# Two attention layers on one core: softmax chain, ends of the halves, offsets and keys one step later in the plan

## The reference

```
xn   = x * bn1_g' + bn1_b
q    = grouped 1x1 conv(xn)                        # 8 groups of 16 channels
off  = tanh(pw(gelu(conv6x6_stride4(q)))) * 4      # 8x8 offsets per group
grid = (8x8 positions + off), scaled
kv   = bilinear sample of xn at grid;  k, v = grouped 1x1 convs of kv
pos  = query grid - key grid;  f = sign(pos) * log1p(|pos|)
bias = relu(relu(f @ w1 + b1) @ w2 + b2) @ w3 + b3 # 2 -> 32 -> 32 -> 1, per query and key
attn = softmax(q k / 4 + bias);  x = x + out_w (attn v) + out_b
x    = x + mlp_w2 gelu(mlp_w1 bn2(x) + mlp_b1) + mlp_b2
```

## Time and profile before

| | us |
|---|---|
| three runs | 893.63, 896.69 (median), 896.9 |
| profiled execution | 898.17 |
| its span, first to last instruction | 896.4 |
| PE, DVE, ACT busy in the span | 811.4, 717.5, 676.1 |
| mean granted TensorE clock | 0.981 of full speed |

### The profile page before, as it was taken

The page is one execution under the profiler, slowest core; times in us unless marked ns, Lnnn a source line. Parts: engine busy times, 40 slices in busy tenths (PEclk is TensorE's granted clock), DMA queues, the critical chain, the costliest instruction groups (busy, mean ns, idle before and its releaser), DMA issues.

```text
span 896.4 us, 27521 instructions
## 1 busy us (share of the span) xinstructions
PE 811.4 (91%) x12470; PEld 232.1 (26%) x12470; DVE 717.5 (80%) x530; ACT 676.1 (75%) x775; POOL 3.1 (0%) x7
## 2 busy tenths in 40 slices
PE   2299998889999999888999999988999999999997
PEld 1122222222222222222222222222222222222224
DVE  4789799798877589898885869979888668989843
ACT  2468778978777688896776877797878678888863
POOL 1000000000000000000000000000000000000000
PEclk8599999999999999999999999999999999999999
DMA  4502010020110201002020200102002020200000
GB/s 163 120 2 49 3 39 12 12 65 3 43 34 1 48 3 49 12 14 54 1 63 15 49 1 14 37 12 56 12 3 61 14 48 2 72 3 3 2 15 24
DMA packets 18264, 27.67 MB, mean 31 GB/s; under 512 B 10980, under 2 KB 11620, under 8 KB 18148
## 3 DMA queue, kind: packets, MB, share of 16 engines
q1 hardware_dynamic: 18148, 25.91, 11.7%
HBM read 23.05 MB, written 2.74 MB: 29 GB/s over the span
## 4 chain that ended last, share of the span: by engine, by line
PE 67%; ACT 15%; DVE 8%; issue 7%; DMA 2%; SPq 1%; ACTq 0%
PE pair L870 23%; PE scores L888 22%; ACT h L467 8%; PE pair L844 6%; DVE h L621 4%; PE pair L1023 3%; PE scores L899 3%; PE pair L978 2%; PE pair L996 2%; PE pair L1014 2%; DVE big L725 2%; PE scores L984 1%; PE pair L923 1%; ACT big L569 1%; ACT L569 1%
## 5 line engine op out<-in xcount | busy, mean ns | idle before, releaser
L621 DVE TENSOR_TENSOR h<-hxy 128x2048 f32<-128x2048 f32 x256 | 578.1, 2287 | 77.2 <-PE pair L870 73.2
L467 ACT ACTIVATE h<-pair 128x1024 f32<-128x1024 f32 x512 | 517.6, 1024 | 143.4 <-PE pair L844 104.6
L870 PE MATMUL pair<-h,wts 32*32 32x512 f32 x8192 | 299.9, 603 | 19.5 <-ACT h L467 5.5
L888 PE MATMUL scores<-h,wts 128*32 128x512 f32 x2048 | 275.6, 607 | 0.1
L844 PE MATMUL pair<-fy,u_rows 32*128 32x512 bf16 x1024 | 102.8, 387 | 15.3 <-DMA fy<-fy_dram 15.3
L870 PEld LDWEIGHTS pair<-h,wts 32*32 32x32 f32 x8192 | 65.9, 103 | 81.2 <-ACT h L467 35.1
L844 PEld LDWEIGHTS pair<-fy,u_rows 32*128 32x128 bf16 x1024 | 26.5, 91 | 232.6 <-issue 232.6
L888 PEld LDWEIGHTS scores<-h,wts 128*32 128x32 f32 x2048 | 42.1, 108 | 157.3 <-issue 148.2
L748 DVE TENSOR_REDUCE neg_max<-pair 128x8 f32<-128x512 f32 x32 | 22.1, 691 | 22.8 <-PE pair L978 22.8
L978 PE MATMUL pair<-const,probs 128*128 128x128 f32 x128 | 20.5, 284 | 21.6 <-ACT h L467 20.8
L477 ACT ACTIVATE probs<-scores,wts 128x512 f32<-128x512 f32 x32 | 22.0, 688 | 23.7 <-PE scores L888 23.5
(11 more groups left out here) (99 smaller groups left out, 341.3 us busy)
## 6 DMA issues: line engine op xcount, KB each, us to landing
hxy<-features_dram SPq DMA_DIRECT2D x64, 256.0 KB, 4.9
wts<-weights_dram SPq DMA_DIRECT2D x2, 960.0 KB, 7.9
att_den<-reciprocals_dram SPq DMA_DIRECT2D x7, 256.0 KB
x<-x_dram SPq DMA_DIRECT2D x2, 512.0 KB, 5.5
fy<-fy_dram SPq DMA_DIRECT2D x16, 64.0 KB
fy_dram<-fy_part SPq DMA_DIRECT2D x24, 32.0 KB, 3.7
out_dram<-x SPq DMA_DIRECT2D x3, 256.0 KB, 5.4
features_dram<-pos_sign SPq DMA_DIRECT2D x4, 128.0 KB, 2.3
```

The source lines that it names most:

```text
L467: emptied("z", 2 * g + j, act.activation(h2[j][g % H2_BUFS][:].rearrange("p r n -> p (r n)"), pair_of("z", 2 * g + j)[:], ACT.Relu))
L621: dve.tensor_tensor(h1[g % H1_BUFS][:].rearrange("p c (y x) -> p c y x", x=W), hx[unit % 2][:, :, t].unsqueeze(2).broadcast_to([128, CT, H ...
L870: ins = pe.matmul(z_of(g, r)[32 * c:32 * (c + 1)], w(l, "w2")[key_rows(r), key_rows(r)], h1[g % H1_BUFS][key_rows(r), c], start=r >= 2, st ...
L888: ins = pe.matmul(scores[phase % 2][32 * r:32 * (r + 1)], w(l, "w3")[:, 32 * t:32 * (t + 1)], h2[rows[0] // 2][step % H2_BUFS][:, r % 2], ...
```

## The change

Numbers in the plan's tables go up by one. The softmax stages move from steps 2, 3, 4 of the following phase to 3, 4, 5 on all three engines; all stages of the end of a half move by one step; of the work for the next segment only `offset`, `offset_tanh` (35 to 36) and `keys_values`, `keys_values_out` (51 to 52) move. `fy_weights` of the second layer moves from DVE step 21 to 22. `copy_scores`, `queries_keys`, `hidden_terms`, the other stages for the next segment, the first segment's own slots and the tail's table keep their steps. No instruction is added or removed, and SP's list of DMAs is the same.

```
-    ("dve", "conv_sum", 1): 34, ("act", "conv_gelu", 0): 33, ("pe", "offset", 0): 35,
-    ("act", "offset_tanh", 0): 35, ("dve", "positions", 0): 38, ("pe", "spread", 0): 37,
+    ("dve", "conv_sum", 1): 34, ("act", "conv_gelu", 0): 33, ("pe", "offset", 0): 36,
+    ("act", "offset_tanh", 0): 36, ("dve", "positions", 0): 38, ("pe", "spread", 0): 37,
...
-    ("pe", "attend", 0): 5, ("act", "attend_out", 0): 5, ("dve", "reciprocal", 0): 9, ("dve", "divide", 0): 12,
+    ("pe", "attend", 0): 6, ("act", "attend_out", 0): 6, ("dve", "reciprocal", 0): 10, ("dve", "divide", 0): 13,
...
-SOFTMAX_SLOTS = {("pe", "scores_t"): 2, ("dve", "score_max"): 4, ("act", "widen_max"): 3,
-                 ("pe", "max_off"): 4, ("act", "exp"): 4}
+SOFTMAX_SLOTS = {("pe", "scores_t"): 3, ("dve", "score_max"): 5, ("act", "widen_max"): 4,
+                 ("pe", "max_off"): 5, ("act", "exp"): 5}
...
-    put("dve", 21, "fy_weights", 1)
+    put("dve", 22, "fy_weights", 1)
```

More of the change, by code:

```diff
@@ L85 @@
     ("dve", "hat_products", 0): 46, ("dve", "hat_products", 1): 47, ("pe", "sample", 0): 48, ("dve", "sample_out", 0): 50,
-    ("pe", "keys_values", 0): 51, ("act", "keys_values_out", 0): 51,
+    ("pe", "keys_values", 0): 52, ("act", "keys_values_out", 0): 52,
 }
 AFTER_SLOTS = {
-    ("pe", "attend", 0): 5, ("act", "attend_out", 0): 5, ("dve", "reciprocal", 0): 9, ("dve", "divide", 0): 12,
-    ("pe", "project", 0): 12, ("dve", "residual1", 0): 14, ("pe", "mlp_up", 0): 14, ("act", "mlp_gelu", 0): 14,
-    ("pe", "mlp_up", 1): 15, ("act", "mlp_gelu", 1): 15, ("pe", "mlp_down", 0): 17, ("dve", "residual2", 0): 19,
-}
-SOFTMAX_SLOTS = {("pe", "scores_t"): 2, ("dve", "score_max"): 4, ("act", "widen_max"): 3,
-                 ("pe", "max_off"): 4, ("act", "exp"): 4}
+    ("pe", "attend", 0): 6, ("act", "attend_out", 0): 6, ("dve", "reciprocal", 0): 10, ("dve", "divide", 0): 13,
+    ("pe", "project", 0): 13, ("dve", "residual1", 0): 15, ("pe", "mlp_up", 0): 15, ("act", "mlp_gelu", 0): 15,
+    ("pe", "mlp_up", 1): 16, ("act", "mlp_gelu", 1): 16, ("pe", "mlp_down", 0): 18, ("dve", "residual2", 0): 20,
+}
+SOFTMAX_SLOTS = {("pe", "scores_t"): 3, ("dve", "score_max"): 5, ("act", "widen_max"): 4,
+                 ("pe", "max_off"): 5, ("act", "exp"): 5}
 TERMS_SLOT = 12
```

## The result

The changed kernel takes 900.22 us, the median of 20 runs (893.73 to 907.11). The kernel before, timed beside it 20 times, takes 896.73 us (893.63 to 899.48). The ratio is 1.004, with an interval of 1.0023 to 1.0057: slower by 3.5 us, with the whole interval above 1, where 889.4, a gain of 7.3, was forecast. The time lies outside the range of 885 to 896 and on the other side.

The account below looks back on a forecast made before the run. PE bounds the kernel, busy 811.4 of 896.4 us, its largest wait in the steps before the scores' transposes. Terms -5.0 + 0 - 0.8 + 0 - 1.5 - 0.9 + 0.5 + 0.4 = -7.3 give 889.4 us, range 885 to 896.

Parts of the forecast that it names:

- plain phases: Transposes one step later see an undisturbed ACT: 0.28 us gained in each of 18 phases, -5.0 us (0 to -8.3).
- L1023 and MLP's first matmuls: MLP's second matmuls inherit the transposes' wait, net 0 in six phases; its first matmuls lose waits, -0.8 us.
- features: Three segments: wait before transposes splits, PE waits some 2.4 us before features instead of 1.1; net 0 (-6.2 to +6.2).
- distances and hats: Three segments: DVE waits 0.7 to 0.8 us for the transposes instead of 1.34; -1.5 us (0 to -3.8).
- second layer's weights: PE's 0.86 us wait for a first layer standing behind these weights goes: -0.9 us (0 to -0.9).
- `q`: Loses the subtraction in front of it and gets a 0.18 us wait, three times: +0.5 us (0 to +0.5).
- DVE's maximum: Comes a step later with more slack behind it, softmax stages keep their distances: counted at nothing.
- tail: Attend of the last-but-one half starts a step later, delaying divide and last reduction: +0.4 us (0 to +2.2).
- clock falls: Rival: every long PE wait drops the clock, 1.7 us each; three falls 892.8 (chance 0.06), nine places 903.0 (0.04).
- I count one such fall before and one after: Clock term: number of half-rate falls in the steps unchanged, 0 us (-1.7 to +5.1, for none and four).
- three falls and 892.8: Rival case: the three longer waits before the features alone drop the clock, two falls more than now; chance 0.06.
- layer2 waiting for DVE's reduction: Listed sign that the forecast is wrong: PE's layer2 held until DVE has done its reduction; no size given.

Follow-up runs that it names:

- e1: Changed kernel plus eight matmuls by zero weights filling PE's wait behind `spread` in each later segment; 899.27 us, ratio 1.0029 to the kernel before.
- e9: Changed kernel with the hidden terms one step later (13), but at step 12 in the three units over the hats; 893.86 us, ratio 0.9962 to before.
- e5: Changed kernel with hidden terms later except at hats, features' exponential behind the features, last-but-one half and its softmax at their old steps; 887.82 us, ratio 0.9885 to before.
- e7: e1 with the last-but-one half and last-but-one phase back at the steps of before; 894.04 us, ratio 0.9958 to the kernel before.
- e11: Changed kernel with only the last-but-one half and last-but-one phase back at the steps of before, no filling; 898.05 us, ratio 1.0019 to before.
- e8: Kernel before plus eight matmuls by zero weights ahead of the transposes behind the offset convolution's GELU, three times; 894.69 us, ratio 0.9975 to before.
- e2: Changed kernel with the hidden terms one step later (13 in place of 12) everywhere; 898.43 us, ratio 1.0011 to the kernel before.
- e3: Changed kernel with `offset` and `offset_tanh` back at step 35; 897.17 us, ratio 1.0013 to the kernel before.
- e4: Changed kernel with offsets and the softmax of the features' and distances' phases in their old slots; 897.67 us, ratio 1.0005 to the kernel before.
- e6: e5 plus eight matmuls by zero weights behind `spread`; 889.35 us, ratio 0.9911 to the kernel before.

## Why the prediction was wrong

Its terms, by phases at full clock (before and e1):

| Term | forecast | measured |
|---|---|---|
| plain phases, 18 | -5.0 | 18 x -0.21 = -3.8 (21.83 to 21.62) |
| L1023 and MLP's first matmuls | -0.8 | -1.0 (phases 65, 73 and 81: 86.43 to 85.88, less a plain phase's 0.21, three times) |
| features | 0 | 3 x +0.10 = +0.3 (28.62 to 28.72) |
| distances and hats | -1.5 | 3 x -0.54 = -1.6 (27.35 to 26.81) |
| second layer's weights | -0.9 | -0.8 (23.22 to 22.18, less 0.21) |
| `q` | +0.5 | 3 x +0.28 = +0.8 (24.71 to 24.78, and the 0.21 that it hides) |
| last phase of the steps | 0 | -0.2 (21.42 to 21.20) |
| DVE's maximum | 0 | 3 x (0.40 + 1.22) = +4.9 |
| sum of the steps | -7.7 | -1.4; measured directly -1.5 |
| tail | +0.4 | +0.5 |
| clock, at the median | 0 | +4.8 |

In the rows of L1023 and `q` the reduction's wait, which e9 and e5 are free of, is taken out and stands in its own row.

*The clock* was the first step to fail. The text knew the mechanism: it had the rival "clock falls", and even a time for nine of them, 903.0. In the profile the clock fell at six of its nine places, at the features and at the transposes of the distances; behind the GELU, where the wait had split into 0.58 and 0.52 us, it did not. The text gave the rival one in ten, since "five of the six waits of 1.65 us and more left the clock up". That reading took waits of 1.65 and 2.05 us for the measure of one of 2.62. The step "I count one such fall before and one after" failed at the size: in the profiled execution it is eight stretches of 3.4 us in these six places, 1.26 us each (10.1 / 8), and 4.8 us at the median. The profiles of e1 and after and the times of e7 and e11 show the cause, since only PE's idle time behind `spread` was filled. The Trainium skill (TensorE: Matmul & The Clock Gate, Part 1: The HAM clock gate) says that the half rate is the default and that activity releases it. The runs agree: none of the six places that e1 and e7 fill dropped the clock, nor the three of e8, while 8 of the 12 waits of 2.62 us in the profiles of after, e2, e9 and e11 (3, 2, 2 and 1 of three each) did. By that rule the text had three falls and 892.8; there were more, since PE was slowed again at the transposes of the distances and two of the falls behind the features lasted 6.8 us. Why a given wait drops the clock in one place and not in the next stays open, and its length is not the whole of it: of the waits of 2.9 us in e3 one of three did.

*The maximum on DVE* was the second. "The maximum on DVE comes a step later too, with more slack behind it": the slack is on the side of its consumer on ACT, but the reduction also empties a PSUM pair, for which layer2 waits. I followed the value and not the buffer. In the new order the reduction had moved past the hidden terms; among the distances I used this to find a gain, and did not look what it does in the other phases. e9 takes back 4.9 us by one slot. This sign was among those that I had listed as wrong: layer2 waiting for DVE's reduction.

*Plain phases* were right in mechanism and in the wait (1.28 behind layer2, forecast 1.27). The gain is 0.21 in place of 0.28, because the step ahead is 0.06 us longer.

*Right* were features (before, PE waited 2.05, 1.11 and 1.02 us there, now 0.58, 0.52 and 2.62; net +0.1 each at full clock), distances and hats (DVE's wait for the transposes is 0.80 in e1 where 0.7 to 0.8 was forecast, though the forecast's own ends, 391.5 and 392.1, give 0.6), L1023 with its 0.29 us of wait (0.38 forecast), the second layer's weights, and the tail's +0.4. But of the tail only the order was priced; a wait of project for the divide comes with it, 0.5 to 1.6 us in the profiles, and the clock falls at it in some executions: in the profiles of e1 (1.59) and e3 (1.05), and 2.6 us behind it in e4 (0.69), but not in those of after (0.71) or e9 (0.73). e1 against e7 puts it at 5.2 us, the order's 0.7 included. Why it falls in one profile and not in another stays open.

Put together: of the 7.7 us forecast for the steps the reduction takes 4.9 and the plain phases 1.2, which, the smaller terms nearly cancelling, leaves the 1.5 measured at full clock; the tail takes 0.5 of it, and the clock's 4.8 make the kernel slower. That features and tail came out near their forecast at full clock does not help the sum: each of the two steps that failed takes more than half of the 7.3 us by itself.

## What to carry to other kernels

When a change gathers short waits of TensorE into one longer wait, do not price the clock behind it by the shorter waits that happened to be harmless, and do not put its fall at one in ten on six of them. Filling the wait, or better moving the work that causes it, tells on the chip whether it is the clock; compare several runs and their mean clock, since one profile can be lucky, and look where else the clock falls. When a stage that empties a PSUM buffer is moved on an in-order engine, list what now stands ahead of it and ask who needs the buffer, beside who needs the value. A slot that is right for one phase can be wrong for another: here the same shift cost 1.4 us at the hats and gained 1.2 at the MLP, and choosing per phase turned a loss of 3.5 us into a gain of 9.

## What the runs showed of the hardware

- The clock falls at a given wait in some places and executions and not in others: at 2.05 us in one of three places before, at 2.62 us in 8 of 12, at 2.9 us in one of three of e3, and in the tail of e4 behind two of 0.69 and 0.78 us, which do not drop it in after. So the same program spreads over 13 us (893.73 to 907.11), and its mean granted clock tells which run one has: 1.3 us for 0.0019.
- A stretch of 3.4 us at 1.2 GHz cost less than half its length here: 1.5 us in before's phase at 161 (30.15 against 28.61), 0.97 in after's hats (27.78 against 26.81), and 0.46 in e5's (27.29 against 26.83). That waits of PE take up the rest is likely but not shown.
- Eight matmuls by zero weights, 1.9 us of PE, went with a clock of 2.4 GHz at every place that they fill: behind `spread` in e1, e6 and e7 (in e6 the wait was short without them) and ahead of the transposes in e8.
